# Blocks of 32 rows in single precision for the experts' rows beyond 128

## The reference

```python
router_logits = x @ w_router                      # 512 x 8
top_w, top_i = jax.lax.top_k(router_logits, 2)
top_w = jax.nn.softmax(top_w)
for ei in range(8):
    hmid = jax.nn.silu(x @ w0[ei]) * (x @ w1[ei])  # 512 -> 1024
    out = out + gating[:, ei:ei + 1] * (hmid @ wo[ei])   # 1024 -> 512
```

## Time and profile before

| | us |
|---|---|
| median of 3 runs | 664.35 |
| lowest, highest | 663.9, 664.51 |
| the profiled execution, device time | 664.46 |
| its span in the trace | 662.7 |
| TensorE busy in the span | 638.7 (96%) |
| VectorE, ScalarE, GpSimd busy | 418.2, 371.4, 244.3 |

### The profile page before, as it was taken

The page is one execution under the profiler, slowest core; times in us unless marked ns, Lnnn a source line. Parts: engine busy times, 40 slices in busy tenths (PEclk is TensorE's granted clock), DMA queues, the critical chain, the costliest instruction groups (busy, mean ns, idle before and its releaser), DMA issues.

```text
span 662.7 us, 10427 instructions
## 1 busy us (share of the span) xinstructions
PE 638.7 (96%) x3741; PEld 523.5 (79%) x3742; DVE 418.2 (63%) x720; ACT 371.4 (56%) x526; POOL 244.3 (37%) x170
## 2 busy tenths in 40 slices
PE   8989999999989999979999999989999999999995
PEld 7867888888867888757788888868888888888884
DVE  7775766658677455666876345762872735763796
ACT  4589998979964344431151254222782736744861
POOL 4159986869893033250000050450022020230213
PEclk9999999999999999999999999999999999999999
DMA  8515544443122512299992322246696472991935
GB/s 315 224 65 196 202 145 161 156 148 123 60 100 82 192 63 96 76 390 385 403 334 70 115 72 88 104 177 251 232 371 236 159 284 100 370 363 37 355 112 167
DMA packets 56071, 125.65 MB, mean 190 GB/s; under 512 B 5208, under 2 KB 5208, under 8 KB 52960
## 3 DMA queue, kind: packets, MB, share of 16 engines
q1 hardware_dynamic: 51584, 115.16, 49.4%
q10 hardware_dynamic: 3168, 5.77, 2.3%
q0 software_dynamic: 1280, 4.20, 2.0%
HBM read 102.31 MB, written 22.81 MB: 189 GB/s over the span
## 4 chain that ended last, share of the span: by engine, by line
PE 80%; DVE 7%; ACT 5%; issue 3%; POOL 3%; DMA 1%; DVEq 1%; ACTq 0%; SPq 0%
PE bank L1496 19%; PE bank L1498 19%; PE bank L1497 19%; PE bank L1510 5%; POOL nat_lo L494 3%; PE bank L1561 3%; PE bank L1529 2%; PE bank L1562 2%; PE bank L1530 2%; PE bank L1958 2%; ACT nat_hi L611 1%; DVE w_lo L1241 1%; PE bank L1737 1%; ACT ct_hi L578 1%; PE bank L1546 1%
## 5 line engine op out<-in xcount | busy, mean ns | idle before, releaser
L494 POOL TENSOR_TENSOR nat_lo<-raw,nat_hi 128x512 fp32r<-128x512 f32 x104 | 136.2, 1338 | 41.8 <-ACT nat_hi L611 41.6
L542 POOL TENSOR_TENSOR e_lo<-e_raw,e_hi 128x2048 fp32r<-128x2048 f32 x8 | 37.4, 4681 | 211.5 <-ACT e_hi L767 211.5
L895 DVE TENSOR_TENSOR ct_lo<-bank,ct_hi 128x512 fp32r<-128x512 f32 x96 | 65.9, 689 | 33.2 <-ACT ct_hi L578 32.5
L1496 PE MATMUL bank<-w_hi,turned 128*128 128x512 f32 x176 | 70.2, 399 | 1.7 <-issue 1.5
L1498 PE MATMUL bank<-w_hi,turned 128*128 128x512 f32 x176 | 68.8, 391 | 0.0
L1497 PE MATMUL bank<-w_lo,turned 128*128 128x512 f32 x176 | 68.6, 390 | 0.0
L611 ACT ACTIVATE nat_hi<-raw 128x512 fp32r<-128x512 f32 x104 | 64.7, 631 | 0.0
L578 ACT ACTIVATE ct_hi<-bank 128x512 fp32r<-128x512 f32 x96 | 56.9, 596 | 9.0 <-PE bank L1510 6.9
L1496 PE MATMUL bank<-e_hi,turned 128*128 128x512 f32 x144 | 58.7, 407 | 1.1 <-issue 1.1
L1510 PE MATMUL bank<-ident,raw 128*128 128x128 f32 x384 | 57.7, 273 | 0.2
L1498 PE MATMUL bank<-e_hi,turned 128*128 128x512 f32 x144 | 56.9, 395 | 0.0
(11 more groups left out here) (283 smaller groups left out, 1439.6 us busy)
## 6 DMA issues: line engine op xcount, KB each, us to landing
raw<-in_ctx_dram SPq DMA_DIRECT2D x24, 1024.0 KB, 5.0
w_raw<-in_L_ffn_w_dram SPq DMA_DIRECT2D x24, 1024.0 KB, 5.3
e_raw<-in_L_ffn_wo_dram SPq DMA_DIRECT2D x16, 1024.0 KB, 7.5
w_raw<-in_L_attn_w_dram SPq DMA_DIRECT2D x8, 1024.0 KB, 5.7
slots_x<-zeros SPq DMA_DIRECT2D x1, 8192.0 KB, 27.6
slots_y<-zeros SPq DMA_DIRECT2D x1, 8192.0 KB, 32.8
e_raw<-in_L_ffn_w_dram SPq DMA_DIRECT2D x8, 1024.0 KB, 7.4
vectors<-slots_x ACTq DMA_DIRECT2D x11, 256.0 KB, 4.9
```

The costliest lines, as they stand in the source:

```text
L494: nc.gpsimd.tensor_tensor(nat_lo[:, j, :], raw[b % 2][:, j, :], nat_hi[:, j, :].bitcast(f32), ALU.subtract).then_inc(nat_lo_ready, 1)
L542: nc.gpsimd.tensor_tensor(e_lo[j][:, :, :], e_raw[j][:, :, :], e_hi[j][:, :, :].bitcast(f32), ALU.subtract).then_inc(e_lo_ready[j], 1)
L895: nc.vector.tensor_tensor(ct_lo[:, n % CR, :], src, ct_hi[:, n % CR, :].bitcast(f32), ALU.subtract).then_inc(t_lo, 1)
L1496: nc.tensor.matmul(dst, lh, rh, start=first and k == 0, stop=False)
```

## The change

An expert's rows beyond 128 are worked in blocks of 32 rows (R = 32) instead of 128, ahead of its last block of 128. Such a short block uses the weights as loaded (`e_raw`), in single precision, without splits: the 32 rows are the stationary operand, and four multiplications (`strips`), one for each quarter of a unit's 512 columns, write to partitions 0 to 31, 32 to 63, 64 to 95 and 96 to 127 of a bank, each through its own strip of 32 columns of the array. Silu, product, hidden copy and output then have 128 columns instead of 512, and one transposition replaces four.

Around this: (1) the row tables are counted in steps of 32, with up to 24 extra blocks, and a block's output is stored in four DMAs. (2) `up` 0 now stands in its own block; the wait for the lowered rows stands ahead of it. (3) The second hidden half is transposed behind the first 3 of the 12 multiplications of the first down half, and the next rows behind that. (4) ScalarE makes the next rows' copies (`next_rows`: an exact one `xgT` of 32 rows and the upper part of 128) behind both hidden halves, ahead of splits 2 and 3; split 4 comes behind the output's copy and split 5 behind the stores. VectorE lowers the next rows behind the second hidden half, ahead of splits 1 to 4. (5) The raw units of the next expert are loaded from the start of the expert's last block (`raw_free`), since the short blocks ahead of it read the raw units. (6) VectorE works out `blocks` and `place_of` ahead of the lowering of the first rows and of split 2. (7) In the very last block the choice matrix and the gates are made ahead of the first lowering. `proj_zero` becomes a step of `fixed_ready`, with no other order.

```diff
-    OV = 7
+    R = 32
+    OV = 24
...
+        xgT = in_last[:, 0, :].rearrange("p (k n) -> p k n", n=R)
+        hmT = [in_last[:, 1 + i, :] for i in range(2)]
...
-            for j in range(2):
-                load_unit(1, j)
...
+            with sp.Fori(1, E) as e:
+                split = [turn_of(e, j) - 1 for j in range(EU)]
                 for j in range(EU):
+                    sp.wait_ge(e_lo_ready[j], split[j])
+                    if j == 0:
+                        sp.wait_ge(raw_free, e)
                     load_unit(e, j)
...
+            def next_rows(b):
+                act.wait_ge(unit_done[3], b + 1)
+                act.wait_ge(xgT_done, b + 1 + KD)
+                rows = bank[7][:, :].rearrange("p (k n) -> p k n", n=P)
+                nc.scalar.activation(xgT[:, :, :], rows[:, :, 0:R], ACT.Copy)
+                nc.scalar.activation(xgT_hi[:, :, :], rows, ACT.Copy).then_inc(xgT_hi_ready, 1)
+                load_rows(b + 2)
...
+            def short_block(b):
+
+                silu(b, 0, P)
+                silu(b, 1, P)
+                whole_hidden(b, 0)
+                next_rows(b)
+                whole_hidden(b, 1)
+                output_copied(b, P)
+                act.wait_ge(y_ready, b + 2)
+                row = row_of(b) * R
+                for q in range(FULL_R):
+                    nc.scalar.dma_start(ys[bass.ds(row, R), q * P:(q + 1) * P], yb[q * R:(q + 1) * R, 0:P]).then_inc(y_stored, 16)
...
+                next_rows(b)
+                split(2)
+                split(3)
+                output_copied(b, D)
+                split(4)
+                act.wait_ge(y_ready, b + 2)
+                row = row_of(b) * R
+                for q in range(FULL_R):
+                    nc.scalar.dma_start(ys[bass.ds(row + q * R, R), :], yb[q * R:(q + 1) * R, :]).then_inc(y_stored, 16)
                 split(5)
...
+            def short_block(b):
+
+                hidden(b, 0, P)
+                hidden(b, 1, P)
+                lower_rows(b + 1)
...
                 hidden(b, 1)
-                if not last:
-                    lower_rows(b + 1)
-                split(1)
                 if last:
-                    gates_made()
                     gathered_added(0)
                 lower_hidden(b, 1)
+                if last:
+                    return
+                lower_rows(b + 1)
+                split(1)
...
+            def strips(dst, left, right, first=True, last=True, begun=None):
+
+                n = len(left)
+                for k in range(n):
+                    for q in range(FULL_R):
+                        mm = nc.tensor.matmul(dst[q * R:(q + 1) * R, 0:P], left[k], right[:, k, q * P:(q + 1) * P],
+                                              start=first and k == 0, stop=last and k == n - 1)
...
+            def short_block(b, e):
+
+                pe.wait_ge(xgT_lo_ready, b + KD)
+                for j in range(3):
+                    short_up(e, j)
+                short_transposed(b, 0)
+                short_up(e, 3)
+                rows_transposed(b + 1)
+                short_transposed(b, 1)
+                pe.wait_ge(y_ready, b + 1)
+                short_down(b, e, 0)
+                short_down(b, e, 1)
+
+            def expert_block(b, e, last=False):
+
+                pe.wait_ge(xgT_lo_ready, b + KD)
+                for j in range(3):
+                    up(e, j)
                 hidden_transposed(b, 0)
                 up(e, 3)
...
+                down_ready(b, e, 0)
+                down_part(0, [0])
                 hidden_transposed(b, 1)
...
+                else:
+                    rows_transposed(b + 1)
+                down_part(0, [1, 2, 3]).then_inc(unit_done[4], 1)
+                down_ready(b, e, 1)
+                down_part(1, [0, 1, 2, 3]).then_inc(unit_done[5], 1)
```

More of the change, by code:

```diff
@@ L859, in _ @@
                 first_upper_rows(k)
-            silu(0, 0)
             act.wait_ge(slots_ready, 5)
@@ L1373, in _ @@
             passed(more)
-            more = mark(nc.vector.scalar_tensor_tensor(extra[:, :], counts, float(3 * P), extra[:, :], ALU.is_gt, ALU.add))
+            more = mark(nc.vector.tensor_reduce(extra[:, :], over, AX.X, ALU.add))
             passed(terms)
@@ L1381, in _ @@
             slots_taken(2)
-            for k in range(KD):
-                first_lower_rows(k)
             passed(more)
@@ L1432, in expert_block @@
                     link(half)
-                lower_hidden(b, 0)
-                if last:
                     for t in range(NT):
@@ L1491, in _, with product @@
         def _(pe):
-            def product(dst, left, right, first=True, last=True):
+            def product(dst, left, right, first=True, last=True, begun=None):
                 n = len(left)
                 for k, ((lh, ll), (rh, rl)) in enumerate(zip(left, right)):
-                    nc.tensor.matmul(dst, lh, rh, start=first and k == 0, stop=False)
+                    mm = nc.tensor.matmul(dst, lh, rh, start=first and k == 0, stop=False)
+                    if k == 0 and begun is not None:
+                        mm.then_inc(begun, 1)
                     nc.tensor.matmul(dst, lh, rl, start=False, stop=False)
```

166 lines of the change are left out of this document (84 added, 82 removed).

## The result

The changed kernel takes 681.72 us (679.11 to 683.62, 4 runs) where the kernel before takes 664.25 in the same session: a ratio of 1.0256, 95% interval 1.0233 to 1.0279. The forecast was 661.7 with a range of 652 to 676. The sign and the range were both missed. The profiled execution took 680.1 us, its span is 678.1.

What follows compares the result with a forecast made beforehand. TensorE, busy 96% of the span, was taken as the bound. Start, full and short blocks summed to 5.1 us gained, the last block 0.7 more: 658.7 us; 3 us for the clock made 661.7, range 652 to 676.

Steps and rivals of the forecast that it cites:

- The strips' price: TensorE's strip multiplications in short blocks: 29 ns a record, taken from quarter-array rows; 5.6 us a short block.
- (a): Rival: strips overlap only in part, 38 ns a record, 3.5 us more, 665 us; chance 0.12.
- (b): Rival: a call's two records fall on one strip and block each other, 58 ns, 674 us; chance 0.13.
- (c): Rival: strips do not overlap, 24 us a short block, 77 us more, 735 us; chance 0.05.
- A short block behind a full one, 11.4 us: Turn at experts 2, 3, 5: late ScalarE work leaves TensorE standing 3.9 us; such a block takes 11.4 us.
- behind a short one, 8.7: Short block following a short one: ScalarE's stores and silu delay the transposition to 4.1 us; 8.7 us together.
- I take a quarter of that, 3 us: TensorE's clock after four rests of about 4 us: a quarter of the 13.6 us bound, 3 us, added.
- (d): Rival: the clock stays low for all of each first short block, 13.6 us more, 672 us; chance 0.06.
- Eight times 0.33 is 2.6 us lost; period 18.25: Full blocks: each waits 0.33 us at the second half's transposition; 2.6 us lost over eight, period 18.25 us.
- hidden by 3 us: Next expert's weights, requested when the full block begins: there at 19 us, last split from 22.1, hidden by 3 us.
- (e): Rival: ScalarE is less late or strips run near 15 ns, 4 to 8 us less, 651 to 655; chance 0.15.
- (f): Rival: weights land late, or ScalarE holds every full block by 1 us, 667 us; chance 0.07.

Runs made afterwards that it cites:

- e9: Changed kernel with silu's table loaded ahead, TensorE filled in its rests, GpSimd's subtraction held back, no short-block branch before the last expert's block: 661.52 us, ratio 0.9948.
- e13: e9 without the seven filling products in each short block; those ahead of the first block stay: 664.70 us, ratio 0.9983.
- e1: Changed kernel with one small extra silu ahead of the expert loop, so its table is already loaded: 673.61 us, ratio 1.0131.
- e3: Changed kernel with the silu of e1 and the filling of e2, 7 filling products in a short block instead of 12: 667.97 us, ratio 1.0039.
- e18: e17 plus GpSimd's subtraction of unit 5 waiting for VectorE's of the next expert's unit 0: 677.12 us, ratio 1.0176.
- e17: Changed kernel without the branch and loop of short blocks ahead of the last expert's full block: 676.37 us, ratio 1.0176.
- e8: e3 without the branch and loop of short blocks ahead of the last expert's full block: 665.70 us, ratio 1.0014.
- e4: Changed kernel with the count of extra blocks forced to zero, leaving eight full blocks and no short ones: 618.42 us, ratio 0.9293.
- e10: e9 with all output stores moved from ScalarE's to SyncE's queue, a full block's behind the next expert's weight loads: 681.80 us, ratio 1.0247.
- e16: Changed kernel with GpSimd's subtraction of unit 5 waiting for VectorE's of the next expert's unit 0: 683.55 us, ratio 1.0264.
- e14: e9 with the fourth unit of strips ahead of a short block's first transposition and no filling in short blocks: 657.20 us, ratio 0.9869.
- e15: e14 with three filling products ahead of the first transposition of each short block: 655.59 us, ratio 0.9837.
- e12: e10 with the fourth unit of strips ahead of a short block's first transposition and no filling in short blocks: 674.39 us, ratio 1.0147.
- e2: Changed kernel with filling products in TensorE's rests, 10 ahead of the first block and 12 in each short block: 674.29 us, ratio 1.0135.
- e7: e3 with GpSimd's subtraction of unit 5 waiting for VectorE's of the next expert's unit 0: 667.46 us, ratio 1.0040.

## Why the prediction was wrong

**The strips' price was right.** TensorE's first 96 strip records of e9, at the full clock:

```profile
440.00 2.83 PE L2020 MATMUL bank<-w_raw,in_last 128*32 128x128 f32 x96 [0.49 <-DVE turned L1371]
```

The next instruction starts at 442.76, so the 96 records cost 2.76 us, 29 ns a record, against 29; where 32 of them stand between transpositions it is up to 32. The quarters of line 1723 and 1737 were the right rows. Rivals (a), (b) and (c) fall with it; the 58 ns of (b) are seen, but as the half clock's price. (A slip in (c): 6 x 24 less 63 is 81 and not 77; nothing hangs on it.)

**A short block behind a full one, 11.4 us, and behind a short one, 8.7: the step that failed.** The list of what ScalarE's queue does at the turn was followed instruction by instruction from the earlier trace rows, but silu was priced at an estimated 0.3 us from a silu that had its table. The diff took the silu ahead of the loop away, and with it the guarantee of the table; the load of 1.28 us stands at the head of each block but the last, in the path of each short one behind another block. With it gone, e13, which has no filling either, shows 8.96 us from short to short at full clock and a rest of 3.18 us behind a full block, against 8.7 and 3.9; e9 has 16.2 from full to short against 16.6. The mechanism was right; a term was missing. The forecast's four pieces of a store and their place in the chain (ScalarE free 3.5 us behind TensorE's last instruction) were real: e13's rest of 1.61 us from short to short stands against the forecast's 1.3 (4.1 less 2.8).

**"I take a quarter of that, 3 us": mis-sized.** The clock cost 7.4 us in the kernel as it is (681.7 to 674.3 with filling) and some 5.6 where the table is loaded ahead (e1 to e3). Rival (d) named the mechanism, and put a bound of 13.6 on it; it had 6%. The only row on it was the trace's end. What it did not hold was how soon the clock returns, and that the longer rests (the table's doing) and the start of the stage feed it too.

**"Eight times 0.33 is 2.6 us lost; period 18.25".** This held wherever nothing else did: 18.25 to 18.27 in e9. The step failed in saying that a full block behind a full one "does not suffer". Two things were passed over. The forecast priced VectorE's splits from a row where GpSimd was silent, and did not ask where the four stores push GpSimd's subtraction. The three rests of 1.36 us cost the kernel as it is nothing measurable (e18 against e17), but 4.2 us once the other causes are gone (e8 to e9). And the last block's turn was priced as before. There the kernel before has a branch with a loop too, without such a rest in its trace; in the kernel after it brings 2.50 us of rest, and e17 puts its price at 5.3 us.

**Weights "hidden by 3 us".** Right for the kernel as it is, where TensorE does not wait for them. e4 and e10 show how thin this cover is: without the first short block, or with a load some 4 us late, TensorE stands 3.6 to 6.5 us.

**The sum.** What the prediction lacked was 20 us. Taken one behind the other, the cures go 681.7 to 668.0 (table and clock; alone they are worth 8.1 and 7.4), to 665.7 (branch), to 661.5 (GpSimd). The order matters, as e16 to e18 show, so these are not four prices but one path. Together the four account for the 20 us. That e9 hits 661.5 is partly chance. The forecast held 3 us for the clock, of which e9's traced execution lost 1.5 in the stage. Against that its first mark comes 1.8 us later than the forecast's and its last step is 1.65 us longer, with a rest of 1.47 us for VectorE. The late mark is not the change's doing: the clock was at half from 285.5 to 295.5 us, in a stage that the change leaves alone, and TensorE is 1.9 us behind e3 from there on. Of the other rivals, (e) has nothing for it, and (f) named the size of the rests in full blocks, about 1 us, with another cause.

## What to carry to other kernels

Where a change moves an activation with a table of its own into a loop or a branch, count a table load at the head of each body, and keep one such activation ahead of the loop. Where it gives TensorE rests of about 2 us and more, put all of TensorE's ready work ahead of what it waits for (here 7.5 us, e13 to e14), fill what is left with products that nobody reads (they also hide what else would show in the rest, as in e10), and count the half clock behind each rest that stays. Where it delays one engine's queue, follow what that queue releases on the others: here four small stores, ahead of ScalarE's last split, moved GpSimd's subtraction onto VectorE's.

## What the hardware showed that was not expected

- Thirteen loads of one table with no other table in between, 1283 ns each.
- TensorE's clock fell to half behind rests of 2.3 us (three of three in e14) and 3.2 us (three of three in e13), and within those of 4.6 us (after), not at those of 1.35 to 1.41 us ahead of the short blocks behind a full one (e9, e15). It is not a sharp rule: a rest of 1.82 us was followed by a fall in e8 and by none in e3, and none followed rests of 2.27 us (e12), 2.50 and 2.90 (after) and 2.92 (e2).
- An empty branch and loop cost 2.5 to 4.6 us of rest, which ended 2.7 to 2.8 us behind the start of a 16 KB instruction load in all eight traces. It was largest (4.59 in e16, 4.64 in e7) where GpSimd's subtraction was late and the load started late.
- VectorE's 2.28 us became 3.11 and 4.44 beside GpSimd's subtraction, and GpSimd's 4.6 became 5.54 where it came second.
